# Softmax sums from TensorE over a block of ones, and one reciprocal and product on VectorE for every two window pairs

## The chip, the cores and the metric

The kernel runs on 1 core of one Trainium2 chip. The metric is the device time of one execution in microseconds (us); of several executions the median is given. Engines are named as the profile names them: PE is TensorE's matrix multiply, PEld its weight load, DVE VectorE, ACT ScalarE, POOL GpSimd, SP SyncE, which here only issues DMAs. Everything is computed in float32.

## The reference, cut to what matters

Sixteen images of 128 channels and 32 x 32 points go through a window-attention block (Swin) and then through a convolution block with Fourier transforms. The attention part, on which the change works:

```python
qkv = (t @ qkv_w.T + qkv_b).reshape(-1, N, 3, NH, hd).transpose(2, 0, 3, 1, 4)
q, k, v = (qkv[0], qkv[1], qkv[2])          # N = 64 tokens of a window, 8 heads, hd = 16
attn = jnp.einsum('whnd,whmd->whnm', q * scale, k)
attn = jax.nn.softmax(attn + bias, axis=-1)
out = jnp.einsum('whnm,whmd->whnd', attn, v).transpose(0, 2, 1, 3).reshape(-1, N, C)
out = out @ proj_w.T + proj_b
...
tok = tok + out
t2 = _ln(tok, ln2_g, ln2_b)
t2 = jax.nn.gelu(t2 @ w1.T + b1, approximate=False) @ w2.T + b2
return tok + t2
```

An image has 16 windows of 64 tokens. The second block is a gelu convolution, a pyramid of dilated convolutions, two axis convolutions, a spectral part (rows, turn, columns, product, inverse) and a gated sum of them, followed by an output convolution.

## The kernel before

Each engine has its own instruction stream, written out by hand in program order; the streams meet only at counting semaphores (`wait_ge` before an instruction, `then_inc` behind one). Nothing reorders them. `swin_rest(0)` does the attention block of image 0 alone. Then `both(n, i)` runs 15 times, with i = n + 1: the convolution block of image n and the attention block of image i, interleaved on every engine. `conv_only` ends the program with the convolution block of image 15.

Attention goes over 8 pairs of windows, j = 0 to 7. For one pair:

- PE `scores` (L518) writes 128 x 512 into PSUM bank 2 or 3: partitions are the 64 queries of two windows, columns 8 heads by 64 keys.
- DVE `bias_max` (L957, L960) adds the bias into `score` (three buffers) and takes the row maxima; POOL `less_max` (L1666) subtracts them; ACT `exponent` (L1382) takes exp.
- DVE `row_sums` (L964, L966) sums each head's 64 numbers and takes the reciprocal of the 8 sums; POOL `widen_inverse` (L1677) repeats each reciprocal 16 times into `inv_wide`.
- PE `prob_transposes` (L529) turns the unnormalised exponentials into bank 0, and ACT `prob_copy` (L1387) copies them into `probT` (two buffers).
- PE `values` (L540) multiplies with the values: 8 matrix products of 64 columns, each of which fills 32 partitions of bank 1, so that bank 1 holds four pairs in 512 columns. With every fourth pair ACT `attention_copy` (L1392) copies bank 1 into `attn_out` (its memory is called xw in the trace).

For each half image (four pairs) PE `spread_inverse` (L551) then turns `inv_wide` into bank 2 or 3, DVE `scale_values` (L972) multiplies `attn_out` with it, and PE `project` applies the output projection. DVE `residual_stats` (L978, L918, L921) adds the residual and takes the statistics of the second layer norm, `norm2` (L926, L929) normalises, and PE goes on with transposes (`n2_transposes`) and the MLP.

In `both`, each of the eight steps j has a piece of the convolution block in it. The pieces that matter here: at j = 5 DVE makes the even product (L1117), from which PE computes `inverse_even` (L467, bank 6 and 7) and then `pyramid_conv` (L647, bank 4 and 5); only then come PE's `values(5)`. At j = 6 DVE's `gate_pyramid` (L1139) reads banks 4 and 5 into py, and PE's `inverse_odd` (L467), which writes the same banks, waits for that (semaphore py_sb). `taps` (L1088, L1090) are VectorE's products of the axis convolutions, one 128 x 1024 instruction each, spread over the steps and, nine of them, behind the attention block.

## Time and profile before

| | us |
|---|---|
| median of 3 runs | 1813.92 |
| lowest and highest of them | 1802.71, 1819.46 |
| the profiled execution's own time | 1805.41 |
| its span, from the first instruction to the last | 1803.6 |
| PE busy in the span | 1549.4 (86%) |
| DVE busy | 1364.0 (76%) |
| ACT busy | 864.2 (48%) |
| POOL busy | 684.9 (38%) |

The span is the part that the trace covers; the profiled execution's own time is 1.8 us more. Busy shares are means over stages with different limits, and no engine is busy throughout. The mean granted TensorE clock was 0.953 of full speed.

### The profile page before, as it was taken

What the parts mean: (1) busy time and instruction counts of PE and PEld (TensorE: products, weight loads), DVE (VectorE), ACT (ScalarE), POOL (GpSimd) and SP (SyncE); (2) the same over time, 40 slices, a digit from 0 to 9 for tenths busy, and PEclk for the clock granted to TensorE, in tenths of its full rate; (3) what the DMA queues carried; (4) which work ended last, traced back from release to release, by engine and by line L of the source; (5) the groups of instructions that cost most, each with busy time, mean ns of one, the idle gap of its engine ahead of it and who ended that gap; (6) DMA issues with size and microseconds to landing.
All of it is one profiled execution on the core that took longest, in us unless ns stands there. A gap on an engine that the chain in (4) does not pass through costs nothing.

```text
span 1803.6 us, 32142 instructions
## 1 busy us (share of the span) xinstructions
PE 1549.4 (86%) x11664; PEld 906.3 (50%) x11664; DVE 1364.0 (76%) x2455; ACT 864.2 (48%) x1380; POOL 684.9 (38%) x603
## 2 busy tenths in 40 slices
PE   5789899888989889888998988889888898988884
PEld 3346455464555546445463554546455464555542
DVE  4558778687777878788687777868788786778866
ACT  2344545455454544545455454544545545454533
POOL 3244251634416244251534416134251623416151
PEclk9899999999999999999999999999999999999997
DMA  4011020111102011020111102011020201102020
GB/s 147 1 26 41 26 52 1 43 33 37 39 23 53 0 37 39 25 51 0 43 33 37 39 23 53 0 37 39 25 51 0 58 18 37 39 12 53 0 54 12
DMA packets 19618, 60.23 MB, mean 33 GB/s; under 512 B 6228, under 2 KB 6228, under 8 KB 19204
## 3 DMA queue, kind: packets, MB, share of 16 engines
q1 hardware_dynamic: 19588, 59.83, 13.7%
q8 instruction: 18, 0.29, 0.1%
q14 instruction: 12, 0.10, 0.0%
HBM read 14.04 MB, written 9.02 MB: 13 GB/s over the span
## 4 chain that ended last, share of the span: by engine, by line
DVE 39%; PE 25%; DVEq 16%; issue 7%; ACT 6%; SPq 4%; DMA 3%; ACTq 1%; POOL 0%; POOLq 0%
DVE hv L1090 16%; DVEq L959 7%; DVE nT L929 5%; PE bank L647 5%; PE bank L674 4%; SPq L428 4%; DVE row_max L960 4%; DVEq L965 3%; PE bank L467 3%; PE bank L518 3%; PE bank L489 2%; DMA k_heads<-kC 2%; PE bank L755 2%; DVE score L957 2%; PE bank L577 1%
## 5 line engine op out<-in xcount | busy, mean ns | idle before, releaser
L674 PE MATMUL bank<-act,mats_sb 128*32 128x512 f32 (+11 forms) x2112 | 267.1, 475 | 1.4 <-DVE xs L1026 1.4
L1666 POOL TENSOR_TENSOR score<-score,row_max 128x512 f32<-128x512 f32 x128 | 133.4, 1042 | 306.7 <-DVE row_max L960 305.1
L1350 ACT ACTIVATE fft<-bank 128x512 f32<-128x512 f32 x224 | 168.9, 807 | 125.7 <-PE bank L467 111.8
L1090 DVE SCALAR_TENSOR_TENSOR hv<-hor,mix,hv 128x1024 f32<-128x1024 f32 x128 | 193.8, 1514 | 10.7
L467 PE MATMUL bank<-cons_sb,fft 128*128 128x128 f32 x1280 | 185.4, 306 | 11.8 <-DVE fft L1117 11.8
L1090 DVE SCALAR_TENSOR_TENSOR hv<-ver,mix,hv 128x1024 f32<-128x1024 f32 x144 | 186.9, 1298 | 11.0
L1382 ACT ACTIVATE score<-score 128x512 f32<-128x512 f32 x128 | 80.8, 631 | 225.8 <-POOL score L1666 225.8
L467 PEld LDWEIGHTS bank<-cons_sb,fft 128*128 128x128 f32 x1280 | 172.7, 217 | 31.4 <-DVE fft L1117 17.0
L1677 POOL COPY inv_wide<-row_inv 128x128 f32<-128x128 f32 x128 | 91.8, 717 | 206.7 <-DVE row_inv L966 206.7
L674 PEld LDWEIGHTS bank<-act,mats_sb 128*32 128x32 f32 x2112 | 117.5, 109 | 99.6 <-issue 81.5
L1696 POOL TENSOR_SCALAR hor<-act,cols_sb 128x1024 f32<-128x1024 f32 x16 | 18.0, 1125 | 391.6 <-ACT act L1407 391.6
L518 PE MATMUL bank<-k_heads,qC 128*64 128x512 f32 x512 | 136.1, 621 | 31.8 <-DMA k_heads<-kC 31.8
L577 PE MATMUL bank<-nC,mats_sb 128*128 128x512 f32 x256 | 127.4, 621 | 38.9 <-ACT nC L1350 23.4
L957 DVE TENSOR_TENSOR score<-bank,rel_bias 128x512 f32<-128x512 f32 x128 | 87.2, 681 | 76.3 <-PE bank L518 76.2
L1387 ACT ACTIVATE probT<-bank 128x512 f32<-128x512 f32 x128 | 77.7, 607 | 101.6 <-PE bank L529 101.3
L1706 POOL TENSOR_SCALAR axis_part<-act,cols_sb 128x320 f32<-128x320 f32 (+1 forms) x128 | 109.4, 855 | 22.5 <-issue 22.5
L587 PE MATMUL bank<-fft,mats_sb 128*128 128x512 f32 x256 | 115.2, 593 | 0.0
L1400 ACT ACTIVATE fft<-bank,fold_b 128x512 f32<-128x512 f32 x128 | 79.2, 689 | 68.5 <-PE bank L577 68.5
L929 DVE TENSOR_SCALAR nT<-xT,mv,rstd 128x128 f32<-128x128 f32 x256 | 104.8, 491 | 3.8
L1708 POOL TENSOR_TENSOR ver<-ver,axis_part 128x320 f32<-128x320 f32 (+1 forms) x64 | 100.8, 1575 | 9.4
L960 DVE TENSOR_REDUCE row_max<-score 128x8 f32<-128x512 f32 x128 | 87.8, 686 | 11.6
L577 PEld LDWEIGHTS bank<-nC,mats_sb 128*128 128x128 f32 x256 | 45.1, 191 | 98.2 <-issue 34.4
(180 smaller groups left out, 2903.9 us busy)
## 6 DMA issues: line engine op xcount, KB each, us to landing
pyr_stack<-pyr SPq DMA_DIRECT2D x192, 144.2 KB, 3.1
x_in<-x_dram SPq DMA_DIRECT2D x16, 512.0 KB, 3.5
k_heads<-kC SPq DMA_DIRECT2D x128, 64.0 KB, 2.4
out_dram<-y_out SPq DMA_DIRECT2D x16, 512.0 KB, 2.8
k_heads<-rel_dram SPq DMA_DIRECT2D x2, 1024.0 KB, 13.0
mats_sb<-mats_dram SPq DMA_DIRECT2D x1, 1978.5 KB, 7.4
z_dram<-z_sb SPq DMA_DIRECT2D x32, 19.1 KB
z_run<-z_dram SPq DMA_DIRECT2D x16, 38.2 KB
```

The source lines that it names most:

```text
L467: last = pe.matmul(dst[:, c * P:(c + 1) * P], src[:, at:at + P], rhs, start=True, stop=True)
L518: last = pe.matmul(bank[2 + j % 2][64 * e:64 * e + 64, :], qC[:, w * WT:(w + 1) * WT], k_heads[:, :, w], start=True, stop=True)
L577: pe.matmul(bank[b][:], w_up[:, f * P:(f + 1) * P], nC[:, HALF * k:HALF * k + HALF], start=True, stop=True).then_inc(up_ps, 1)
L587: last = pe.matmul(bank[b][:], w_down[:, f * P:(f + 1) * P], hidden[:, f, HALF * k:HALF * k + HALF], start=False, stop=(f == FC - 1))
L674: last = pe.matmul(grids[32 * d:32 * d + 32, y0 - 16 * k:y1 - 16 * k, x0:x1], w_pyr[:, d, t], act[:, y0 + dy:y1 + dy, x0 + dx:x1 + dx], st ...
L929: last = dve.tensor_scalar(nT[:, c], source[:, c], mv[:, c, 0:1], rstd[:, c:c + 1], ALU.subtract, ALU.mult)
L957: dve.tensor_tensor(score[:, j % 3].rearrange("p h k -> p (h k)"), bank[2 + j % 2][:], rel_bias[:], ALU.add).then_inc(s_biased, 1)
L959: dve.drain()
L960: dve.tensor_reduce(row_max[:, j % 3], score[:, j % 3], AX.X, ALU.max).then_inc(s_max, 1)
L1090: last = dve.scalar_tensor_tensor(hv[:], src, mix[:, a, k:k + 1], hv[:], ALU.mult, ALU.add)
L1350: return act_.activation(dst, src, ACT.Copy)
L1666: pool.tensor_tensor(score[:, j % 3], score[:, j % 3], row_max[:, j % 3].unsqueeze(2).broadcast_to([P, HEADS, WT]), ALU.subtract)\
```

## The change

TensorE computes the softmax sums itself. A constant block `pair` (128 x 32) has ones where the row and the column belong to the same head of a head pair. Behind the 8 value products of a pair stand 4 more products over this block, each of 128 columns, from the same `probT`. Each gives the sum of a head's exponentials, repeated over that head's 16 rows, in the layout of the values. Bank 1 now holds two pairs: columns 0 to 255 the values and columns 256 to 511 the sums.

`scale_values` reads both halves of the bank, once for every two pairs (q = 0 to 3): a reciprocal of 128 x 256 from PSUM into the new tile `inverse`, a drain, and a product of 128 x 256 into `attn_out`. It stands in steps j = 2, 4 and 6 (for q = 0, 1, 2), and for q = 3 behind the residual of the first half. `values` of an even pair waits for the scaling that empties the bank.

`row_sums`, `widen_inverse`, `spread_inverse` and `attention_copy` are gone, with their semaphores. The image loop, the convolution block and the DMAs are as they were.

```diff
             def values(i, j):
                 pe.wait_ge(pT_sb, 8 * i + j + 1)
-                if j == 4:
-                    pe.wait_ge(o_sb, 2 * i + 1)
+                if j % 2 == 0 and j > 0:
+                    pe.wait_ge(o_scaled, 4 * i + j // 2)
+                at = (j % 2) * P
                 for e in range(2):
                     w = 2 * j + e
                     for g in range(HP):
-                        last = pe.matmul(bank[1][32 * g:32 * g + 32, (w % 8) * WT:(w % 8 + 1) * WT],
-                                         v_pair[:, w, g].rearrange("p e d -> p (e d)"),
-                                         probT[:, j % 2, g, e * WT:(e + 1) * WT], start=True, stop=True)
+                        pe.matmul(bank[1][32 * g:32 * g + 32, at + e * WT:at + (e + 1) * WT],
+                                  v_pair[:, w, g].rearrange("p e d -> p (e d)"),
+                                  probT[:, j % 2, g, e * WT:(e + 1) * WT], start=True, stop=True)
+                for g in range(HP):
+                    last = pe.matmul(bank[1][32 * g:32 * g + 32, 2 * P + at:2 * P + at + P], con("pair"),
+                                     probT[:, j % 2, g], start=True, stop=True)
                 last.then_inc(o_ps, 1)
...
-            def row_sums(i, j):
-                dve.wait_ge(s_exp, 8 * i + j + 1)
-                dve.tensor_reduce(row_sum[:, j % 3], score[:, j % 3], AX.X, ALU.add)
-                dve.drain()
-                dve.reciprocal(row_inv[:, j], row_sum[:, j % 3]).then_inc(s_inv, 1)
-
-            def scale_values(i, k):
-                dve.wait_ge(iv_ps, 2 * i + k + 1)
-                dve.wait_ge(o_sb, 2 * i + k + 1)
-                h = slice(HALF * k, HALF * k + HALF)
-                dve.tensor_tensor(attn_out[:, h], bank[2 + k][:], attn_out[:, h], ALU.mult).then_inc(o_scaled, 1)
+            def scale_values(i, q):
+
+                dve.wait_ge(o_ps, 8 * i + 2 * q + 2)
+                dve.reciprocal(inverse[:], bank[1][:, 2 * P:4 * P])
+                dve.drain()
+                dve.tensor_tensor(attn_out[:, 2 * P * q:2 * P * q + 2 * P], bank[1][:, 0:2 * P], inverse[:], ALU.mult)\
+                   .then_inc(o_scaled, 1)
...
                 for j in range(PAIRS):
                     if j + 2 < PAIRS:
                         bias_max(i, j + 2)
-                    row_sums(i, j)
+                    if j in (2, 4, 6):
+                        scale_values(i, j // 2 - 1)
                     if j == 0:
                         route_weights(n)
-                    if j == PAIRS - 1:
-                        scale_values(i, 0)
                     conv_slot(n, j)
                     if j == 3:
                         r_even_bias(n)
                 residual_stats(i, 0)
-                scale_values(i, 1)
+                scale_values(i, 3)
```

The order of the instructions, at the places that the prediction speaks of. First DVE at the end of step j = 5 and in steps 6 and 7, in the loop over images. Names after the arrow are tiles; what a row waits for stands in brackets. Before:

```order
L1090 SCALAR_TENSOR_TENSOR hv<-hor,mix,hv 128x1024
L964 TENSOR_REDUCE row_sum<-score 128x8 [waits s_exp]
L966 RECIPROCAL row_inv<-row_sum 128x8
L1139 SCALAR_TENSOR_TENSOR py<-bank4,cols_sb,axis_part 128x512 [waits pyc_ps,pyramid_mixed,cut_sb]
L1139 SCALAR_TENSOR_TENSOR py<-bank5,cols_sb,axis_part 128x512 [waits pyc_ps]
L1090 SCALAR_TENSOR_TENSOR hv<-hor,mix,hv 128x1024 x2
L964 TENSOR_REDUCE row_sum<-score 128x8 [waits s_exp]
L966 RECIPROCAL row_inv<-row_sum 128x8
L972 TENSOR_TENSOR xw<-bank2,xw 128x512 [waits o_sb,iv_ps]
```

Now:

```order
L1073 SCALAR_TENSOR_TENSOR hv<-hor,mix,hv 128x1024
L952 RECIPROCAL inverse<-bank1 128x256 [waits o_ps]
L954 TENSOR_TENSOR xw<-bank1,inverse 128x256
L1122 SCALAR_TENSOR_TENSOR py<-bank4,cols_sb,axis_part 128x512 [waits pyc_ps,pyramid_mixed,cut_sb]
L1122 SCALAR_TENSOR_TENSOR py<-bank5,cols_sb,axis_part 128x512 [waits pyc_ps]
L1073 SCALAR_TENSOR_TENSOR hv<-hor,mix,hv 128x1024 x4
L961 TENSOR_TENSOR xT<-bank2,resT 128x512 [waits res_sb,proj_ps]
```

The reciprocal and the product of q = 2, which wait for `values` of pairs 4 and 5 (o_ps), stand ahead of the two `gate_pyramid` rows (py). The sums of j = 6 and 7 and the 512-wide product on xw are gone.

Then DVE behind step 7, where the residual of the first half image (xT with bank 2) and the second layer norm are. Before:

```order
L978 TENSOR_TENSOR xT<-bank2,resT 128x512 [waits res_sb,proj_ps]
L918 BN_STATS stats<-xT 128x6 x4
L921 BN_AGGR mv<-stats 128x2 x4
L972 TENSOR_TENSOR xw<-bank3,xw 128x512 [waits o_sb,iv_ps]
L926 RECIPROCAL rstd<-std 128x4 [waits ln2_std]
L929 TENSOR_SCALAR nT<-xT,mv,rstd 128x128 x4
L978 TENSOR_TENSOR xT<-bank3,resT 128x512 [waits res_sb,proj_ps]
L918 BN_STATS stats<-xT 128x6 x4
```

Now:

```order
L961 TENSOR_TENSOR xT<-bank2,resT 128x512 [waits res_sb,proj_ps]
L905 BN_STATS stats<-xT 128x6 x4
L908 BN_AGGR mv<-stats 128x2 x4
L952 RECIPROCAL inverse<-bank1 128x256 [waits o_ps]
L954 TENSOR_TENSOR xw<-bank1,inverse 128x256
L913 RECIPROCAL rstd<-std 128x4 [waits ln2_std]
L916 TENSOR_SCALAR nT<-xT,mv,rstd 128x128 x4
L961 TENSOR_TENSOR xT<-bank3,resT 128x512 [waits res_sb,proj_ps]
```

The product from bank 3 has become the reciprocal and the product of q = 3, at the same place, which waits for o_ps.

Last PE from the end of `pyramid_conv` into step 6. Before:

```order
L647 MATMUL bank5<-pyr_stack,mats_sb 32x512 x12
L540 MATMUL bank1<-probT,v_pair 32x64 [waits pT_sb]
L540 MATMUL bank1<-probT,v_pair 32x64 x7
L467 MATMUL bank4<-cons_sb,fft 128x128 [waits py_sb]
L467 MATMUL bank4<-cons_sb,fft 128x128 x3
L467 MATMUL bank5<-cons_sb,fft 128x128 [waits py_sb]
L467 MATMUL bank5<-cons_sb,fft 128x128 x3
L529 MATMUL bank0<-cons_sb,score 128x128 [waits pT_sb,s_exp]
L529 MATMUL bank0<-cons_sb,score 128x128 x3
L551 MATMUL bank2<-cons_sb,inv_wide 128x128 [waits s_biased,iv_wide]
L551 MATMUL bank2<-cons_sb,inv_wide 128x128 x3
L459 MATMUL bank6<-cons_sb,fft 128x128 [waits ae_sb]
```

Now:

```order
L640 MATMUL bank5<-pyr_stack,mats_sb 32x512 x12
L538 MATMUL bank1<-probT,v_pair 32x64 [waits pT_sb]
L538 MATMUL bank1<-probT,v_pair 32x64 x7
L542 MATMUL bank1<-probT,cons_sb 32x128 x4
L464 MATMUL bank4<-cons_sb,fft 128x128 [waits py_sb]
L464 MATMUL bank4<-cons_sb,fft 128x128 x3
L464 MATMUL bank5<-cons_sb,fft 128x128 [waits py_sb]
L464 MATMUL bank5<-cons_sb,fft 128x128 x3
L526 MATMUL bank0<-cons_sb,score 128x128 [waits pT_sb,s_exp]
L526 MATMUL bank0<-cons_sb,score 128x128 x3
L456 MATMUL bank6<-cons_sb,fft 128x128 [waits ae_sb]
```

Four products of 128 columns follow the values of the pair, and the four products of `spread_inverse` (bank 2, inv_wide) are gone. `inverse_odd` (banks 4 and 5 from fft) still waits for py_sb.

## Rows read from the trace of the kernel before

**Rows 1.** The page's chain that ended last: by engine, by line.

```profile
DVE 39%; PE 25%; DVEq 16%; issue 7%; ACT 6%; SPq 4%; DMA 3%; ACTq 1%; POOL 0%; POOLq 0%
DVE hv L1090 16%; DVEq L959 7%; DVE nT L929 5%; PE bank L647 5%; PE bank L674 4%; SPq L428 4%; DVE row_max L960 4%; DVEq L965 3%; PE bank L467 3%; PE bank L518 3%; PE bank L489 2%; DMA k_heads<-kC 2%; PE bank L755 2%; DVE score L957 2%; PE bank L577 1%
```

**Rows 2.** The waits: who waited for whom, total us, times, longest.

```profile
DVE py L1139 <- PE bank L647: 83.0, 32, 4.1
```

**Rows 3.** Two stretches of one image: busy us of PE, PEld, DVE, ACT, POOL; then clock.

```profile
782.00:812.00 30.00, 25.98 (x232) 15.84 (x232) 27.96 (x44) 14.02 (x23) 17.32 (x16) 0.98 0.26 59
812.00:822.80 10.80, 10.79 (x85) 6.06 (x86) 4.84 (x7) 3.56 (x4) 0.40 (x2) 0.74 0.00 0
```

**Rows 4.** Timeline of DVE in that image: start, duration, line, operation, count.

```profile
810.61 1.35 DVE L1117 TENSOR_TENSOR fft<-fft 128x1024 f32<-128x1024 f32 x1
...
819.60 0.75 DVE L1139 SCALAR_TENSOR_TENSOR py<-bank,cols_sb,axis_part 128x512 f32<-128x512 f32 x1 [4.02 <-PE bank L647]
822.08 0.75 DVE L1139 SCALAR_TENSOR_TENSOR py<-bank,cols_sb,axis_part 128x512 f32<-128x512 f32 x1 [1.73 <-PE bank L647]
822.92 2.64 DVE L1090 SCALAR_TENSOR_TENSOR hv<-hor,mix,hv 128x1024 f32<-128x1024 f32 x2
...
826.46 0.69 DVE L972 TENSOR_TENSOR xw<-bank,xw 128x512 f32<-128x512 f32 x1
827.24 4.43 DVE L1090 SCALAR_TENSOR_TENSOR hv<-hor,mix,hv 128x1024 f32<-128x1024 f32 x2
831.59 0.68 DVE L978 TENSOR_TENSOR xT<-bank,resT 128x512 f32<-128x512 f32 x1
...
833.61 0.66 DVE L972 TENSOR_TENSOR xw<-bank,xw 128x512 f32<-128x512 f32 x1
...
835.51 0.69 DVE L978 TENSOR_TENSOR xT<-bank,resT 128x512 f32<-128x512 f32 x1
```

**Rows 5.** Timeline of PE in that image, matrix products alone.

```profile
812.01 3.78 PE L467 MATMUL bank<-cons_sb,fft 128*128 128x128 f32 x16 [1.02 <-DVE fft L1117]
815.72 6.29 PE L647 MATMUL bank<-pyr_stack,mats_sb 96*32 96x512 f32 x48
821.83 0.40 PE L540 MATMUL bank<-probT,v_pair 128*32 128x64 f32 x16
822.16 2.05 PE L467 MATMUL bank<-cons_sb,fft 128*128 128x128 f32 x16
...
824.49 1.06 PE L551 MATMUL bank<-cons_sb,inv_wide 128*128 128x128 f32 x8
...
829.86 1.06 PE L467 MATMUL bank<-mats_sb,xw 128*128 128x128 f32 x8
```

**Rows 6.** DVE's instruction groups by shape, whole span: busy us, mean ns.

```profile
L964 DVE TENSOR_REDUCE row_sum<-score 128x8 f32<-128x512 f32 x128 | 86.6, 677 | 0.2 <-ACT score L1382 0.2
...
L994 DVE TENSOR_SCALAR xm<-bank,cols_sb 128x256 f32<-128x256 f32 x64 | 26.7, 477 | 17.0 <-PE bank L587 17.0
...
L966 DVE RECIPROCAL row_inv<-row_sum 128x8 f32<-128x8 f32 x128 | 26.0, 203 | 9.4
...
L926 DVE RECIPROCAL rstd<-std 128x4 f32<-128x4 f32 x32 | 5.5, 173 | 5.8 <-ACT std L1346 5.8
...
L926 DVE RECIPROCAL rstd<-std 128x8 f32<-128x8 f32 x16 | 3.3, 204 | 6.6 <-ACT std L1342 6.6
...
L1066 DVE RECIPROCAL vec<-vec 128x1 f32<-128x1 f32 x16 | 2.6, 164 | 1.2
```

**Rows 7.** One-microsecond stretches around that image, columns as in rows 3.

```profile
773.00:774.00 1.00, 0.00 (x0) 0.00 (x0) 1.00 (x1) 0.30 (x1) 1.00 (x1) 1.00 0.57 94
775.00:776.00 1.00, 1.00 (x6) 0.29 (x4) 0.18 (x1) 0.00 (x0) 0.00 (x0) 1.00 0.00 0
871.00:872.00 1.00, 0.12 (x1) 0.12 (x2) 0.82 (x3) 0.00 (x0) 0.85 (x2) 1.00 0.00 0
873.00:874.00 1.00, 1.00 (x3) 0.82 (x4) 0.00 (x0) 0.32 (x1) 0.83 (x2) 0.50 0.00 0
```

54 lines of the change are left out of this document (10 added, 44 removed).

## The prediction

> **What bounds the kernel now.** I read the chain that ended last first. VectorE holds the largest part of it, 39%, with 16% more in its queue (DVEq, mostly drains that wait for the instruction before them); TensorE has 25% [rows 1]. So both matter, and the question is where each leads. The stretches of one image answer it. From 782 to 812 us, steps j = 0 to 5, VectorE is busy 27.96 of 30 us and TensorE 25.98 [rows 3]: VectorE leads, TensorE has 4.0 us to spare. From 812 to 822.8 it is the other way: TensorE is busy throughout and VectorE 4.84 of 10.8 us [rows 3]. The timelines show why. `even_product` starts at 810.61 and TensorE starts `inverse_even` on it at 812.01, then `pyramid_conv` until about 822 [rows 4, 5]. VectorE has little to do meanwhile and waits 4.02 and 1.73 us for the two halves of the pyramid in `gate_pyramid` [rows 4]. Over the program this wait is 83.0 us in 32 waits, two in each of 16 images, so the one image stands for all [rows 2]. Behind it VectorE leads again: its rows to 835.51 follow each other without a gap to speak of [rows 4]. Work on VectorE thus costs time before 810.6 and after 822, and is free between.
>
> **The price of one new scaling.** It is a reciprocal of 256 elements per partition from PSUM, a drain, and a product of 256. The product has a near row: 477 ns for a tensor-scalar of 256 elements out of PSUM [rows 6]; I take 0.45 us. The reciprocal has none of its size. Three of other widths exist: 164 ns for 1 element, 173 for 4, 203 to 204 for 8 [rows 6]. The step from 4 to 8 is 31 ns, 7.7 ns per element, where the row sum takes 677 ns for 512 elements, 1.3 ns each with everything in it [rows 6]. The step from 1 to 4 is only 3 ns per element, so a start-up hides the pace in small ones. At 7.7 ns the reciprocal is 204 + 248 x 7.7 = 2.1 us. The low end of this reading is the mean slope from 1 to 8, 5.7 ns, which gives 1.6 us; the far low end is the pace of the others, 0.45 us (a rival below). The high end is a slope that still grows, 8.5 ns: 2.3 us. I take 2.1, because the widest pair of rows is nearest to 256. One scaling is then S = 2.1 + 0.05 + 0.45 = 2.6 us, with ends 2.1 and 2.8.
>
 The three rows lean towards it, but no row here has a reciprocal long enough to show it.
>
> **What is removed on VectorE.** Eight row sums and reciprocals of 0.68 + 0.20 = 0.88 us [rows 6], 7.0 us per image, and two products of 512, 0.69 and 0.66 us [rows 4]: 8.4 us. Four scalings add 10.4. By totals VectorE gets 2.0 us more per image; by place it is worse.
>
> **Steps 0 to 5.** Six row sums go, 5.3 us, and two scalings come (q = 0 in j = 2, q = 1 in j = 4), 5.2 us. Both wait for values that TensorE finished one step before, so they don't wait. `even_product` starts as it did: 0.0. TensorE has a new wait here: `values(2)` and `values(4)` wait for these scalings, and the next `scores` is queued behind them, for which the next `bias_max` waits. VectorE has other work between (two taps in step 2, `boosted` in step 4), of about the length of `values` and `scores`, so I cost it at nothing; without that cover it would be up to 1 us at each. The added sums on TensorE are 512 columns like the value products, which take 0.40 us for the eight [rows 5]. Half as many instructions, so I take 0.3 us each step, between 0.25 and 0.4. It lies in TensorE's spare 4.0 us.
>
> **The hole at 812 to 822.** Here the change hurts. The sums of pair 6 lay in the hole. What stands there now, the scaling of q = 2, waits for `values(5)`, which TensorE issues only behind `pyramid_conv`: 821.83 + 0.40 + 0.3 = 822.5. And `gate_pyramid` is queued behind the scaling, though its first half was ready at 819.60 [rows 4]. So VectorE idles to 822.5, scales until 825.1, and gates until 826.8 (0.75 us each and a gap), where it ended at 822.83. TensorE's `inverse_odd` waits for the first gate, 825.9, and began at 822.16 [rows 5]: +3.8 us, in which TensorE stands. It gets back `spread_inverse`, 0.89 us from its start to that of the next piece (1.06 with the overlap) [rows 5], and pays 0.3 for the sums of pair 6: project(0), 829.86 to about 830.9 [rows 5], ends at 834.1. VectorE has by then done its taps: 826.8 + 2.64 + 4.43 = 833.8 [rows 4]. The residual of the first half, 831.59 before, starts at 834.1: **+2.5 us**. Two row sums less on VectorE there don't show, as TensorE is the later one.
>
> **Behind it.** Between this residual and the second one stood a product of 0.66 us; now a whole scaling, 2.6, and the second projection waits for it. **+2.0 us.** The second residual thus starts 4.5 us late, and all that follows on both engines hangs on it. The ScalarE copy and `spread_inverse` of the second half, which are gone, lay beside other work there. POOL's `widen_inverse` was on no chain (POOL has 0% of it [rows 1]), so its removal is worth 0.
>
> **The clock.** After idle stretches the granted clock falls to its lower level: TensorE did nothing in 773 to 774 and had full clock at 775, but after 871 to 872, nearly idle, it had 0.50, 1.2 GHz, at 873 [rows 7]. So the same kind of wait is followed by a fall at one time and not at another. What a fall costs is in the timeline: `inverse_even` at the lower level took 3.78 us for 16 records and `inverse_odd` at the upper 2.05 for as many [rows 5]. A fall after the new 3.5 us wait would hit `inverse_odd` and the turns behind it, 3 us of work, so up to +3.0 us in the image. Ends 0 and 3.0; I take 1.5, as the rows show both outcomes.
>
> **Sum.** 15 images with both blocks: 15 x (2.5 + 2.0 + 1.5) = 90 us. Image 0 alone has the same four scalings with less beside them. There the wait of `values(2)` is bare, 2.6 us, the sums add 8 x 0.3, and two `spread_inverse` go: I take +4, with ends 0 and 8. The last block has no attention. 1805.4 + 94 = 1899 us for an execution like the profiled one. The median of the runs is 0.5% above that one (1813.92 to 1805.41), so **1908 us**.
>
> **Rivals.**
> - *The reciprocal is as quick as other instructions* (0.45 us, S = 0.95). Steps 0 to 5 lose 5.3 and gain 1.9, but TensorE has just 4.0 us to give, less 1.8 for six groups of sums, so `even_product` comes 2.2 us early. The gap then costs 0.7 (values and sums) + 0.95 + 0.83 until the first gate, which lands at 822.1, as before; 0.6 us come back by `spread_inverse`, 0.3 go for q = 3. Minus 0.3 to 0.5 per image: 1807 us, not slower than before. It decides at S of about 1.1. If TensorE's denser work in steps 0 to 5 also kept the clock up in `inverse_even` and `pyramid_conv` (0.74 granted in 812 to 822.8 [rows 3]), another 2.7 us per image would go: 1766. For it: nothing in the rows but that the product has this pace. Against it: 31 ns for four elements. The Trainium skill's cycle table (same page, on the errata of SBUF sources) gives VectorE 120 cycles and one per element out of PSUM whatever the operation; by that rule the reciprocal would be 0.39 us, and the rows 4 and 8 elements wide speak against it. 8% for 1807, 4% for 1766.
> - *A slope of 5.7 ns.* S = 2.1: 0.5 less at q = 2 and at q = 3, and up to 1.0 less before the even product. 15 x 4.0 + 4: about 1878. 10%.
> - *The clock falls in every image, and S is 2.8.* 15 x (4.5 + 0.4 + 3.0) + 8 = 127 us: 1941. For it: the wait is the longest of TensorE in the image. 22%.
> - *The four sum products don't run side by side on the array* and take 1.0 us, as 4 of the 128-column products of `spread_inverse` do. 0.7 more at pairs 5, 6 and partly 7: +1.5 us per image, 1931. Against it: eight value products take 0.40 [rows 5]. 5%.
>
> **How the numbers follow.** Forecast 45%, between 1885 and 1925; the rivals as above, 49%; 6% for a gain that I don't see, of one or two per cent. 1850 to 1948 leaves out the quick reciprocal, the unseen gain and the tail of the clock case, some 18% to 20%. A change within 1% can't be told from none here, the runs before differ by 0.9%. Faster by over 1%: 0.06. Within 1%: 0.11. Slower: 0.83.
>
> **What would show it.** In the new profile the 128 x 256 reciprocal should have a mean of 2.1 us (1.6 to 2.3), 64 of them, and the sums 0.3 us a group. VectorE's wait in step 6 should have moved from py to the reciprocal, end with `values(5)`, and TensorE should wait some 3.5 us for py ahead of `inverse_odd`. `even_product` should stand at the same distance from the first `scores`. The prediction is wrong if the reciprocal takes under 1 us, or if TensorE reaches project(0) late by less than 2 us though the reciprocal is long.

## The result, and the profile after

| | before | after |
|---|---|---|
| median, us | 1814.86 | 1939.55 |
| lowest and highest of 4 runs each | 1802.71, 1819.46 | 1930.09, 1947.91 |
| the profiled execution's own time, and its span | 1805.41, 1803.6 | 1937.6, 1935.7 |
| mean granted clock | 0.953 | 0.935 |

The ratio is 1.069 (1.063 to 1.076): the change costs 125 us. The direction was right and the time lies in the range, 32 us above the forecast of 1908 and 8 below the range's upper end. A fourth execution of the kernel before has moved its median from 1813.92 to 1814.86.

The page of the changed kernel: the engines' busy time, and the chain that ended last, by engine and by line.

```profile
PE 1581.2 (82%) x12432; PEld 909.5 (47%) x12432; DVE 1439.5 (74%) x2295; ACT 839.3 (43%) x1348; POOL 665.0 (34%) x475
...
PE 44%; DVE 24%; DVEq 10%; ACT 8%; issue 7%; SPq 3%; DMA 3%; ACTq 1%; POOLq 0%; POOL 0%
PE bank L570 8%; PE bank L464 7%; PE bank L580 6%; DVE nT L916 6%; PE bank L640 4%; DVEq L946 4%; PE bank L515 4%; PE bank L667 4%; SPq L425 3%; PE bank L456 3%; DVE row_max L947 3%; DVE inverse L952 3%; DVEq L953 3%; DVE hv L1073 2%; DMA k_heads<-kC 2%
```

The chain has gone over to TensorE, 44% where it had 25% [rows 1], and its first entry is L570, the MLP's first product (L577 before). TensorE didn't get that much more work, 1581 us against 1549. It waits for VectorE more often (the waits below), and what follows such waits runs in part at a lower clock: the same 256 products of that line took a mean of 621 ns before and take 789 now.

VectorE's groups after, as in [rows 6]: busy us, mean ns of one, idle time before them.

```profile
L952 DVE RECIPROCAL inverse<-bank 128x256 f32<-128x256 f32 x64 | 111.6, 1744 | 86.4 <-PE bank L542 86.4
...
L954 DVE TENSOR_TENSOR xw<-bank,inverse 128x256 f32<-128x256 f32 x64 | 27.2, 425 | 5.1 <-issue 0.4
...
L916 DVE TENSOR_SCALAR nT<-xT,mv,rstd 128x128 f32<-128x128 f32 x256 | 135.6, 611 | 3.8
```

The reciprocal takes 1.74 us, not 2.1, and the product 0.43: a scaling is S = 2.2 us. The third group is one that the prediction didn't look at. The normalisation, L929 before, took 104.8 us with a mean of 491 ns; the same 256 instructions now take 135.6.

The waits after: who waited for whom, total us, times, longest.

```profile
DVE inverse L952 <- PE bank L542: 86.4, 16, 9.0
...
PE bank L464 <- DVE py L1122: 45.6, 15, 3.0
...
PE bank L538 <- DVE xw L954: 40.1, 31, 3.2
...
PE bank L464 <- DVE xw L954: 31.4, 16, 4.3
```

The wait of [rows 2] for the pyramid has gone from py to the reciprocal: 16 waits, one of them in image 0, where no pyramid stands ahead, and one in each of the 15 other images, for `values(5)` with its sums. The others are new, all of TensorE for VectorE: 3.0 us per image ahead of `inverse_odd` (L464 <- py), and others for a scaling.

The gap of one image after, VectorE's timeline, which answers to [rows 4]:

```profile
882.76 1.76 DVE L952 RECIPROCAL inverse<-bank 128x256 f32<-128x256 f32 x1 [5.15 <-PE bank L542]
884.60 0.42 DVE L954 TENSOR_TENSOR xw<-bank,inverse 128x256 f32<-128x256 f32 x1
884.94 1.40 DVE L1122 SCALAR_TENSOR_TENSOR py<-bank,cols_sb,axis_part 128x512 f32<-128x512 f32 x2
886.43 7.31 DVE L1073 SCALAR_TENSOR_TENSOR hv<-hor,mix,hv 128x1024 f32<-128x1024 f32 x4
895.51 0.69 DVE L961 TENSOR_TENSOR xT<-bank,resT 128x512 f32<-128x512 f32 x1 [1.77 <-PE bank L464]
...
897.53 1.73 DVE L952 RECIPROCAL inverse<-bank 128x256 f32<-128x256 f32 x1
...
899.92 3.14 DVE L916 TENSOR_SCALAR nT<-xT,mv,rstd 128x128 f32<-128x128 f32 x4
```

And TensorE's, which answers to [rows 5]:

```profile
858.48 0.43 PE L538 MATMUL bank<-probT,v_pair 128*32 128x64 f32 x16 [0.22 <-DVE xw L954]
...
870.37 0.43 PE L538 MATMUL bank<-probT,v_pair 128*32 128x64 f32 x16 [2.02 <-DVE xw L954]
870.62 0.40 PE L542 MATMUL bank<-probT,cons_sb 128*32 128x128 f32 x8
870.95 1.08 PE L515 MATMUL bank<-k_heads,qC 128*64 128x512 f32 x4
...
874.91 2.05 PE L464 MATMUL bank<-cons_sb,fft 128*128 128x128 f32 x16 [0.34 <-DVE fft L1100]
876.90 5.36 PE L640 MATMUL bank<-pyr_stack,mats_sb 96*32 96x512 f32 x48
882.07 0.41 PE L538 MATMUL bank<-probT,v_pair 128*32 128x64 f32 x16
882.30 0.40 PE L542 MATMUL bank<-probT,cons_sb 128*32 128x128 f32 x8
885.73 2.79 PE L464 MATMUL bank<-cons_sb,fft 128*128 128x128 f32 x16 [3.04 <-DVE py L1122]
...
899.81 1.16 PE L464 MATMUL bank<-mats_sb,xw 128*128 128x128 f32 x8 [1.78 <-DVE xw L954]
903.12 0.66 PE L456 MATMUL bank<-cons_sb,nT 128*128 128x128 f32 x4 [2.15 <-DVE nT L916]
904.55 5.46 PE L570 MATMUL bank<-nC,mats_sb 128*128 128x512 f32 x6 [0.78 <-ACT nC L1332]
```

Read together: VectorE stands 5.15 us until the sums of pair 5 are there, scales, and only then gates the pyramid; `inverse_odd` begins at 885.73, after 3.04 us of waiting. This is what the prediction described. The second place is at 899.92: four normalisations take 3.14 us.

The clock, in the columns of [rows 3] and [rows 7]:

```profile
845.03:875.03 30.00, 26.07 (x266) 16.04 (x264) 28.13 (x36) 11.76 (x20) 15.12 (x10) 1.00 0.26 59
875.03:885.83 10.80, 7.76 (x89) 3.79 (x89) 5.49 (x7) 3.75 (x5) 0.73 (x1) 1.00 0.00 0
...
887.00:888.00 1.00, 1.00 (x7) 1.00 (x6) 0.93 (x2) 1.00 (x1) 1.00 (x1) 0.50 0.00 0
...
905.00:906.00 1.00, 1.00 (x2) 0.36 (x2) 0.56 (x5) 0.89 (x2) 0.00 (x0) 0.50 0.00 0
```

In the gap of this image the clock is now full, 1.00 where it was 0.74 [rows 3], and `inverse_even` takes 2.05 us where it took 3.78 [rows 5]. TensorE waited 0.34 us ahead of it, where it had waited 1.02 [rows 5]. It falls later: to 0.50, 1.2 GHz, at 887 behind the new wait, and at 905 behind the waits for `xw` and `nT`. There the six products of L570 take 5.46 us; their like before, at full clock, took 2.81.

**Where it went, by stretches.** The table cuts an image at instructions that every kernel here has, and gives the mean length of each stretch over the 15 images with both blocks ("tail" and "image": over the 14 that have a next one). "Start" is from the first `scores` to `even_product`, "pyramid" to the end of `pyramid_conv`, "gate" to the end of `gate_pyramid`, "res 1" and "res 2" to the start of the two residuals, "axes" to the first gating of the axis convolutions, "tail" to the next image's first `scores`. It is worked out from the start and end of these instructions in the traces, one execution of each kernel. The kernels e1 to e11 are told below.

| us per image | start | pyramid | gate | res 1 | res 2 | axes | tail | image |
|---|---|---|---|---|---|---|---|---|
| before | 35.90 | 10.88 | 0.83 | 8.75 | 3.93 | 16.20 | 31.65 | 108.2 |
| after | 37.42 | 9.17 | 4.08 | 8.96 | 7.49 | 16.19 | 32.71 | 116.1 |
| e1, copy in place of the reciprocal | 35.38 | 9.57 | 2.75 | 8.14 | 4.19 | 16.20 | 32.51 | 108.8 |
| e2, gate first | 37.28 | 8.89 | 0.82 | 8.20 | 7.49 | 16.19 | 31.76 | 110.7 |
| e3, GpSimd's sum of squares later | 37.97 | 9.33 | 4.09 | 8.87 | 5.56 | 16.20 | 32.34 | 114.4 |
| e4, e2 and e3 | 37.46 | 9.70 | 0.82 | 8.20 | 5.52 | 16.20 | 32.41 | 110.4 |
| e5, sums twice | 38.12 | 8.83 | 4.31 | 9.11 | 7.49 | 16.19 | 33.70 | 117.7 |
| e6, after with 15 reciprocals in the set-up | 37.93 | 9.40 | 4.09 | 8.95 | 7.48 | 16.18 | 33.24 | 117.5 |
| e7, inverse on ScalarE | 40.54 | 9.79 | 0.82 | 9.10 | 5.68 | 16.36 | 32.99 | 115.3 |
| e8, e1 and e2 | 35.82 | 9.78 | 0.82 | 8.19 | 4.19 | 16.20 | 31.96 | 107.0 |
| e9, e4 and a dead reduce | 39.91 | 10.91 | 0.82 | 8.22 | 5.52 | 16.25 | 33.07 | 114.7 |
| e10, before with sums ahead | 37.84 | 10.80 | 0.83 | 8.75 | 3.92 | 16.19 | 30.82 | 109.2 |
| e11, halves | 38.20 | 10.07 | 0.82 | 8.59 | 4.65 | 16.24 | 31.47 | 109.9 |

After minus before is +1.5, -1.7, +3.3, +0.2, +3.6, 0, +1.1: 7.9 us per image, 119 us in 15. Image 0, to the first `scores` of image 1, is 10.9 us longer (137.2 against 126.3). Together 130 of the 132 us between the spans.

**What of it is the clock.** The granted clock falls in some images and not in others, so the same two traces tell most of it apart:

| us | at full clock from end to end | the other images |
|---|---|---|
| start, before | 35.9 (10 images) | 35.9 (5) |
| start, after | 37.0 (11) | 37.3 to 39.4 (4) |
| pyramid, before | none | 10.1 to 11.5 (15) |
| pyramid, after | 8.6 (11) | 9.8 to 12.5 (4) |
| res 1, before | 8.75 (15) | none |
| res 1, after | 8.06 (4) | 9.2 to 10.2 (11) |

So the start is 1.1 us longer without any fall of the clock, and falls add 0.5 in the mean. `res 1` is 0.7 us shorter without a fall, which costs 1.1 us in 11 of the 15 images. "Gate" and "res 2" hardly differ from image to image, whatever the clock. The tail's shortest is 30.8 us in both kernels, and its mean is what falls of the clock in and ahead of it add.

Image 0 after, TensorE's timeline (matrix products of the values and of `project`, L464):

```profile
60.60 0.50 PE L538 MATMUL bank<-probT,v_pair 128*32 128x64 f32 x16 [3.24 <-DVE xw L954]
...
70.60 0.43 PE L538 MATMUL bank<-probT,v_pair 128*32 128x64 f32 x16 [3.24 <-DVE xw L954]
...
78.05 0.65 PE L538 MATMUL bank<-probT,v_pair 128*32 128x64 f32 x16 [1.88 <-DVE xw L954]
...
88.29 2.08 PE L464 MATMUL bank<-mats_sb,xw 128*128 128x128 f32 x8 [4.34 <-DVE xw L954]
```

Nothing covers a scaling there: TensorE waits 12.7 us for the four. `project` takes 2.08 us for the eight records that take 1.06 in [rows 5].

### The profile page after: what moved, and what is told of

Read it like the earlier page. It is cut to its first block, busy times and chain, and to the rows that moved or that the text cites. A ratio compares the mean times of both kernels' runs of the same rounds, so it can differ in the third digit from the quotient of the medians.

```text
span 1935.7 us, 33148 instructions
## 1 busy us (share of the span) xinstructions
PE 1581.2 (82%) x12432; PEld 909.5 (47%) x12432; DVE 1439.5 (74%) x2295; ACT 839.3 (43%) x1348; POOL 665.0 (34%) x475
## 4 chain that ended last, share of the span: by engine, by line
PE 44%; DVE 24%; DVEq 10%; ACT 8%; issue 7%; SPq 3%; DMA 3%; ACTq 1%; POOLq 0%; POOL 0%
PE bank L570 8%; PE bank L464 7%; PE bank L580 6%; DVE nT L916 6%; PE bank L640 4%; DVEq L946 4%; PE bank L515 4%; PE bank L667 4%; SPq L425 3%; PE bank L456 3%; DVE row_max L947 3%; DVE inverse L952 3%; DVEq L953 3%; DVE hv L1073 2%; DMA k_heads<-kC 2%
## 5 line engine op out<-in xcount | busy, mean ns | idle before, releaser
L1638 POOL TENSOR_TENSOR score<-score,row_max 128x512 f32<-128x512 f32 x128 | 184.7, 1443 | 364.8 <-DVE row_max L947 362.7
L464 PE MATMUL bank<-cons_sb,fft 128*128 128x128 f32 x1280 | 178.8, 298 | 50.0 <-DVE py L1122 45.6
L1073 DVE SCALAR_TENSOR_TENSOR hv<-hor,mix,hv 128x1024 f32<-128x1024 f32 x128 | 205.0, 1601 | 10.4
L464 PEld LDWEIGHTS bank<-cons_sb,fft 128*128 128x128 f32 x1280 | 164.2, 208 | 74.3 <-DVE py L1122 49.6
L570 PE MATMUL bank<-nC,mats_sb 128*128 128x512 f32 x256 | 166.9, 789 | 38.9 <-ACT nC L1332 23.4
L952 DVE RECIPROCAL inverse<-bank 128x256 f32<-128x256 f32 x64 | 111.6, 1744 | 86.4 <-PE bank L542 86.4
L667 PEld LDWEIGHTS bank<-act,mats_sb 128*32 128x32 f32 x2112 | 117.5, 109 | 99.6 <-issue 81.4
L916 DVE TENSOR_SCALAR nT<-xT,mv,rstd 128x128 f32<-128x128 f32 x256 | 135.6, 611 | 3.8
L1332 ACT ACTIVATE nC<-bank 128x512 f32<-128x512 f32 x64 | 38.2, 597 | 207.6 <-PE bank L456 207.6
L1680 POOL TENSOR_TENSOR py<-py,xm 128x1024 f32<-128x1024 f32 x16 | 53.2, 3326 | 190.4 <-DVE py L1122 190.4
L570 PEld LDWEIGHTS bank<-nC,mats_sb 128*128 128x128 f32 x256 | 57.7, 243 | 118.0 <-issue 59.6
L1378 ACT ACTIVATE fft<-bank,fold_b 128x512 f32<-128x512 f32 x128 | 80.1, 688 | 74.4 <-PE bank L570 74.2
```

The lines of the kernel that those rows point to most:

```text
L464: last = pe.matmul(dst[:, c * P:(c + 1) * P], src[:, at:at + P], rhs, start=True, stop=True)
L570: pe.matmul(bank[b][:], w_up[:, f * P:(f + 1) * P], nC[:, HALF * k:HALF * k + HALF], start=True, stop=True).then_inc(up_ps, 1)
L667: last = pe.matmul(grids[32 * d:32 * d + 32, y0 - 16 * k:y1 - 16 * k, x0:x1], w_pyr[:, d, t], act[:, y0 + dy:y1 + dy, x0 + dx:x1 + dx], st ...
L916: last = dve.tensor_scalar(nT[:, c], source[:, c], mv[:, c, 0:1], rstd[:, c:c + 1], ALU.subtract, ALU.mult)
L952: dve.reciprocal(inverse[:], bank[1][:, 2 * P:4 * P])
L1073: last = dve.scalar_tensor_tensor(hv[:], src, mix[:, a, k:k + 1], hv[:], ALU.mult, ALU.add)
```

## The experiments

### e1 and e2: is it the length of the reciprocal, or its place?

e1_copy puts a copy of the same block where the reciprocal stood (the division is left out: the values are multiplied by the sums):

```diff
-                dve.reciprocal(inverse[:], bank[1][:, 2 * P:4 * P])
+                dve.tensor_copy(inverse[:], bank[1][:, 2 * P:4 * P])
```

> The changed kernel with the reciprocal of 128 x 256 replaced by a copy of the same block into the same tile, so the division is left out and the output is not scaled. Three theories. (P, place) The loss comes from where the scalings of q = 2 and q = 3 stand: the copy takes 0.42 us where the reciprocal takes 1.74, so 1.3 us go at q = 2, 1.3 at q = 3, up to 1.4 ahead of the even product and perhaps 1 of the clock; the wait of gate_pyramid for values(5) stays. 4 to 5 us per image: 1865 to 1880 us. (L, length) The loss is the reciprocal's length and nothing else: all of it goes, 1815 us or less. (S, sums) The loss is the added products on TensorE: next to nothing changes, 1920 to 1940.

Measured: 1823.03 us, ratio to the kernel before 1.005 (1.002 to 1.008). The copy in e1_copy, from VectorE's groups:

```profile
L952 DVE COPY inverse<-bank 128x256 f32<-128x256 f32 x64 | 26.3, 411 | 92.9 <-PE bank L542 92.9
```

1.33 us less at each of four scalings are 5.3 us per image, and the image got 7.3 shorter: 2.0 in the start, 1.3 in the gate, 0.8 up to the first residual, 3.3 up to the second and 0.2 in the tail, against 0.4 more in the pyramid. So the price by place (1865 to 1880, mine) was wrong, and the theory that all hangs on the length came near. What gives more than its own 1.3 us is the stretch to the second residual, taken up in e3. TensorE's wait for py is still there, 1.7 us in each of the 15 images: a quick inverse alone brings the kernel to half a per cent above the time before, not below it.

e2_gate_first leaves the arithmetic and moves the scaling of q = 2 behind `gate_pyramid`:

```diff
             def conv_slot(n, j, i=None):
...
                 elif j == 6:
                     gate_pyramid(n)
+                    if i is not None:
+                        scale_values(i, 2)
...
-                    if j in (2, 4, 6):
+                    if j in (2, 4):
                         scale_values(i, j // 2 - 1)
```

> The changed kernel with the scaling of q = 2 moved behind gate_pyramid in step 6. Same instructions, same work. Place: gate_pyramid ends 0.8 us behind pyramid_conv as before the change (4.1 now), TensorE's 3.0 us wait for py goes and the fall of the clock behind it with it; 3.3 to 4 us per image, 1880 to 1890 us. Length or sums: nothing is gained by a move, 1930 to 1940, as the scaling only stands 1.6 us later.

Measured: 1856.44 us, ratio 1.025 (1.020 to 1.030). The reciprocal's wait has gone, from 86.4 us to 0.9, as VectorE's groups in e2_gate_first show:

```profile
L952 DVE RECIPROCAL inverse<-bank 128x256 f32<-128x256 f32 x64 | 111.5, 1742 | 0.9 <-PE bank L542 0.9
```

The waits of the same kernel have the one for the pyramid back, with the count of [rows 2]:

```profile
DVE py L1122 <- PE bank L640: 67.9, 32, 3.8
```

The gate stretch is 0.82 us again, as before the change, and the image 5.4 us shorter: 3.3 there, 0.8 up to the first residual, where the clock now stays full in all 15 images, and 0.95 in the tail. This is two thirds of the loss, from one line's place, and more than the 50 to 60 us that I expected. That the length or the sums alone are to blame falls with this run.

e1 says 7.3 us per image and e2 5.4, of 7.9 in all. They don't add, since a short instruction at the wrong place and a long one at the right place each do little harm. e8 below does both.

### e3 and e4: the slow normalisation

The normalisation of the first half (899.92 above) overlaps with GpSimd's instruction of `square_sum`, whose timeline row is:

```profile
900.07 2.39 POOL L1687 TENSOR_TENSOR fft<-fft 128x1024 f32<-128x1024 f32 x1 [10.13 <-ACT fft L1444]
```

One of VectorE's four instructions there took 2.37 us and ended with it. Before, this `square_sum` ran at 836.14 to 838.49 beside the second half's statistics, behind the normalisation at 834.42 that [rows 4] leaves out; the longer scaling has pushed the normalisation onto it. e3_square_late makes GpSimd wait until the normalisation of the first half is done:

```diff
-            def square_sum(n):
+            def square_sum(n, i=None):
+                if i is not None:
+                    pool.wait_ge(n2T_sb, 2 * i + 1)
```

> The changed kernel with one wait more on GpSimd: its sum of squares (128 x 1024, 2.4 us) waits for the first norm2 of the image. In the changed kernel one of the four 128 x 128 normalisations takes 2.37 us where it took 0.3, and ends when GpSimd's sum of squares ends. If the two collide, the four take 1.1 us again instead of 3.1 and the second residual starts 2.0 us earlier: 30 us, 1905 to 1912. Rival: the long normalisation has another cause (the reciprocal ahead of it), then it stays at 2.4 us and the time at 1930 to 1940.

Measured: 1908.89 us, ratio 1.053 (1.050 to 1.057). The normalisation in e3_square_late:

```profile
L916 DVE TENSOR_SCALAR nT<-xT,mv,rstd 128x128 f32<-128x128 f32 x256 | 105.3, 493 | 3.8
```

It has its 493 ns again, the second residual comes 1.9 us earlier per image, and the median is 30.7 us lower, as expected. So of the +3.6 us in that stretch 1.9 are the collision, and the rest is about what the longer scaling costs by itself (2.17 in place of 0.66 is 1.5). The Trainium skill ("SBUF — State Buffer", Who interferes with whom) says that VectorE and GpSimd share one pair of ports as an exclusive lock, and that a tensor-scalar on SBUF can be among those that contend. The trace agrees, with 2.37 us for one instruction of 128 x 128 that ends with GpSimd's.

e4_both_orders has the edits of e2 and e3.

> Both moves together: the scaling of q = 2 behind gate_pyramid, and GpSimd's sum of squares behind the first norm2. Place: the gains add, 5.5 to 6 us per image, 1850 to 1858 us. What is then left against the kernel before is image 0 (some 11 us), 1.6 us per image for the longer scaling of q = 3, and 1.4 us ahead of the even product, less what the clock gives. Rival: if the clock falls at another place in their stead, or one hides the other, it stays above 1875.

Measured: 1852.35 us (1833.70 to 1856.96), ratio 1.019 (1.014 to 1.025). The time is within what I expected, but the 2 us at the second residual, which are there in the table, gave only 0.3 per image over e2, and 4 us by the medians: the pyramid is 0.8 us longer and the tail 0.65. Image 0, in which e4 and e2 are the same, ends 3.6 us later (141.9 against 138.3). The mean clock of the profiled execution is 0.940 against 0.951 in e2, so other falls of the clock have eaten the gain there. That is one execution: the profiled one is the slowest of e4's four, and the fastest, 1833.70 us, had a clock of 0.958. What the second move adds to the first is thus open within some 20 us.

### e5 and e6: the price of the sums, and of a reciprocal

e5_double_sums issues the four sum products of a pair twice:

```diff
-                for g in range(HP):
+                for g in range(2 * HP):
+                    g = g % HP
```

> The changed kernel with each of the four sum products issued twice, the second over the first, so the result is the same. In the changed kernel the sums of a pair put the next product 0.33 us later or less. Place: only the pairs with TensorE ahead of VectorE feel it (5, 6 and 7), 0.25 us each, some 0.7 us per image: 1945 to 1955 us. Sums as a cause of the loss: 8 x 0.3 us per image or more, 1975 us and above.

Measured: 1977.10 us (1966.22 to 1992.82), ratio 1.093 (1.085 to 1.101), 37 us more than the changed kernel by the medians, and 29 by the spans. A group of four products costs 0.33 us in the changed kernel from its start to the next piece (882.30 above follows 882.07; at 870.62 the next `scores` begins at 870.95). Eight groups in 16 images are then 42 us of TensorE time. The table's stretches show 1.6 us more per image, 24 us, and image 0 ends 7.3 us later. How much of that is the sums' own time the totals can't say. e6 below leaves the loop over the images as it was in the changed kernel, and its one execution took 1968.47 us, with 1.4 us more per image and a mean clock of 0.922. That is what falls of the clock can do to a kernel with the same loop, and nearly as much as e5's total.

What is left of e5 without the clock is small. The shortest start is 37.20 us where it was 36.88, the gate is 4.31 in every image where it was 4.08, and `res 1` at full clock is 8.27 where it was 8.06. These are 0.2 to 0.3 us at each of three places, 0.8 us per image, about what I had expected for the place. (The tail's 1.0 us more can't be told apart in this way.) So the prediction's "lies in TensorE's spare 4.0 us" holds nearly: in the start a doubled group in each step costs 0.3 us.

e6_widths puts reciprocals of several widths at the start of the program, each followed by a drain, from SBUF (`boost`) and from PSUM (`bank`), once each:

```diff
+            for width in (1, 2, 4, 6, 8, 12, 16, 32, 64, 128, 256):
+                dve.reciprocal(inverse[:, 0:width], wide[:, 0:width])
+                dve.drain()
```

> The changed kernel with 15 more reciprocals in the set-up, each alone behind a drain: from SBUF at 1, 2, 4, 6, 8, 12, 16, 32, 64, 128 and 256 elements per partition, from PSUM at 1, 8, 64 and 128. It measures the disputed price by itself. The prediction took 7.7 ns an element from the step between 4 and 8 wide; the 256 wide one took 1.74 us. Theory one: a start-up of some 0.2 us and a constant 6.2 ns an element, so 64 wide 0.55 us, 128 wide 0.95, and the source makes no difference but some 50 ns. Theory two: PSUM as a source slows it, then 256 from SBUF differs from 1.74 by more than 0.1 us.

The groups of VectorE in that stretch of e6_widths:

```profile
L1293 DVE RECIPROCAL inverse<-boost 128x256 f32<-128x256 f32 x1 | 1.8, 1753 | 0.1
L1296 DVE RECIPROCAL inverse<-bank 128x128 f32<-128x128 f32 x1 | 1.0, 957 | 0.1
L1293 DVE RECIPROCAL inverse<-boost 128x128 f32<-128x128 f32 x1 | 1.0, 952 | 0.1
...
L1293 DVE RECIPROCAL inverse<-boost 128x64 f32<-128x64 f32 x1 | 0.6, 553 | 0.1
...
L1293 DVE RECIPROCAL inverse<-boost 128x8 f32<-128x8 f32 x1 | 0.2, 202 | 0.1
...
L1293 DVE RECIPROCAL inverse<-boost 128x4 f32<-128x4 f32 x1 | 0.2, 177 | 0.1
```

From 64 elements to 128 it takes 399 ns more, from 128 to 256 801: 6.2 to 6.3 ns per element, and SBUF and PSUM differ by 5 ns. From 4 to 8 the step is 25 ns here, 6.25 each, where [rows 6] gave 31: these rows have means over different places, and a difference of two start-up-bound rows magnified 62 times was a weak base. The Trainium skill ("VectorE: DVE Perf Modes", First, the fixed hardware budget) gives a repeat count of 8, which I had read as 8 cycles per element. By its 0.96 GHz the measured pace is 6.0 cycles, so that reading was a third too high.

### e7 and e8: another way to the inverse, and the change with a quick one

e7_ln_exp computes the inverse on ScalarE, as exp(-ln(sum)), with the gate first as in e2:

```diff
+            def invert(i, q):
+                act_.wait_ge(o_ps, 8 * i + 2 * q + 2)
+                act_.activation(inverse[:], bank[1][:, 2 * P:4 * P], ACT.Ln)
+                act_.drain()
+                act_.activation(inverse[:], inverse[:], ACT.Exp, scale=-1.0).then_inc(inv_sb, 1)
```

> The inverse moves to ScalarE: log of the sums from PSUM, then exp of its negative into the same tile, at the end of steps 1, 3, 5 and 7; VectorE keeps the 256 wide product, and the scaling of q = 2 stands behind gate_pyramid. Full computation. VectorE loses 4 x 1.8 us per image. ScalarE gains 4 pairs of activations and 8 table loads of 1.28 us, as log and the other functions are not in one table. Place: the even product comes up to 2 us earlier than in the changed kernel, and behind the residual the inverse is ready at about the time at which the scaling ended; less than the kernel with gate_pyramid first (1856), 1825 to 1850 us. Rival: ScalarE's loads hold up the copies that TensorE waits for, 1870 us or more.

Measured: 1926.26 us, ratio 1.063 (1.058 to 1.068), where the rival in it had put it (1870 or more). ScalarE's groups at these two lines in e7_ln_exp:

```profile
L1375 ACT ACT_TABLE_LOAD x64 | 82.1, 1283 | 1.2
L1377 ACT ACT_TABLE_LOAD x64 | 82.1, 1283 | 3.3
L1377 ACT ACTIVATE inverse<-inverse 128x256 f32<-128x256 f32 x64 | 26.7, 417 | 0.7
L1375 ACT ACTIVATE inverse<-bank 128x256 f32<-128x256 f32 x64 | 24.6, 384 | 64.5 <-PE bank L543 64.2
```

And who waits for the inverse there, from its waits:

```profile
DVE xw L953 <- ACT inverse L1377: 91.1, 61, 5.4
```

The two functions take 0.80 us, the loads of their tables 2.57: one inverse is 3.4 us, longer than on VectorE, and VectorE waits for it. The rival's mechanism is there too: in the same view TensorE waits 74.4 us for ScalarE's copies at L457 and 40.6 for `probT`, where e2 has 24.7 and 11.3. The start alone is 3.3 us longer than in e2.

e8_copy_gate combines e1 and e2 (again a copy, the division left out).

> The copy in the place of the reciprocal (the division is left out) and the scaling of q = 2 behind gate_pyramid. It bounds what the change could give if the inverse were as quick as other instructions. Place: the two causes, order and length, add in part: from 1856 some 2 us per image go ahead of the even product and 1.3 to 3.3 behind the residual, 1780 to 1800 us, below the kernel before. Length alone: the order gives nothing once the instruction is short, 1815 to 1823.

Measured: 1788.97 us (1778.43 to 1800.45 of 7 runs), ratio 0.987 (0.983 to 0.991), as expected. With the gate first, the reciprocal's length alone costs 3.7 us per image (e2 to e8 in the table). This is the one version that is faster than the kernel before, and it lacks the division. So the form of the change is worth 1.3% if the inverse is as short as a copy and stands behind the gate. It loses its gain because the 128 x 8 reciprocals of the kernel before, 0.20 us for a pair, have become 128 x 256, 1.74 us for two.

### e9 to e11: what stood beside GpSimd's subtraction

The prediction had 0.0 for the start, where 1.5 us were lost, 1.1 of them at full clock. The page shows another group that changed, with not one instruction of it edited: `less_max` on GpSimd. Its group in the changed kernel:

```profile
L1638 POOL TENSOR_TENSOR score<-score,row_max 128x512 f32<-128x512 f32 x128 | 184.7, 1443 | 364.8 <-DVE row_max L947 362.7
```

In the kernel before all 128 took 1041 to 1045 ns. GpSimd subtracts right after the row maxima, and VectorE's next work was then the row sum, beside which the subtraction took no longer. In the changed kernel the next work in steps 1, 3 and 5 is a product of tiles in SBUF, and there both take longer. In steps 2 and 4 it is the reciprocal. Three subtractions in a row after, from GpSimd's timeline:

```profile
968.74 2.38 POOL L1638 TENSOR_TENSOR score<-score,row_max 128x512 f32<-128x512 f32 x1 [0.24 <-DVE row_max L947]
...
972.94 1.04 POOL L1638 TENSOR_TENSOR score<-score,row_max 128x512 f32<-128x512 f32 x1
978.89 2.10 POOL L1638 TENSOR_TENSOR score<-score,row_max 128x512 f32<-128x512 f32 x1 [4.91 <-DVE row_max L947]
```

They alternate: 45 of the 128, three in each of 15 images, take over 2 us. VectorE pays as well. Its instructions in the start apart from the row sums and the scalings are the same in both kernels, and by the traces they are busy 27.0 us per image before and 28.8 after. The Trainium skill ("SBUF — State Buffer", Who interferes with whom) says of trn2 that a tensor-reduce never contends with GpSimd and that a VectorE instruction with two inputs in SBUF does: the trace agrees in both.

e10_before_swap is the kernel before with nothing but the order changed, the row sums ahead of the maxima of the next pair, so that a product follows the maxima:

```diff
-                    if j + 2 < PAIRS:
-                        bias_max(i, j + 2)
                     row_sums(i, j)
+                    if j + 2 < PAIRS:
+                        bias_max(i, j + 2)
```

> The kernel before the change with one swap in the loop over images: the row sums of pair j stand ahead of bias_max of pair j + 2, not behind it. Same instructions. Cover: GpSimd's subtraction now runs beside the products of the convolution block, its mean rises from 1.04 towards 1.4 us, and the even product comes 1 to 2 us later: 1825 to 1845 us. Rival: no cover, the order does not matter, 1805 to 1820 us.

Measured: 1827.83 us, ratio 1.010 (1.005 to 1.016). The subtraction's group in e10_before_swap:

```profile
L1666 POOL TENSOR_TENSOR score<-score,row_max 128x512 f32<-128x512 f32 x128 | 184.9, 1445 | 314.7 <-DVE row_max L960 314.7
```

It has the mean of the changed kernel, and the start is 1.9 us longer (37.84 against 35.90); in 14 of the 15 images the clock is full there up to the last microsecond. VectorE's instructions, the same ones, are busy 2.5 us longer in it, so this is not an engine that waits because of the new order. In step 2, where a 128 x 1024 tensor-scalar of a tap now follows the maxima, the subtraction keeps its 1.04 us and the tap takes 1.54 instead of 0.89: GpSimd's mean shows only a part of such a cost. This shows the cover in the kernel that the change started from.

e9_cover puts it back into e4 the other way: a row sum of `score`, whose result nobody uses, follows the maxima in steps 1, 3 and 5.

```diff
+                    if j in (1, 3, 5):
+                        dve.wait_ge(s_exp, 8 * i + j + 1)
+                        dve.tensor_reduce(row_sum[:, j % 3], score[:, j % 3], AX.X, ALU.add)
+                        dve.drain()
```

> The kernel with both moves (gate_pyramid first, sum of squares late) and, in steps 1, 3 and 5, a sum over the exponentials that nobody reads, put back at the place where the row sum stood. In the changed kernel GpSimd's subtraction of the maxima takes 2.0 to 2.4 us in these steps and 1.04 in the steps where the reciprocal follows the maxima; before the change it took 1.04 in all 128. Theory (cover): VectorE's row sum stood beside the subtraction and does not collide with it, the products on SBUF tiles that stand there now do. Then the subtraction takes 1.04 us again, the products lose some 0.6 us each, and three dead sums of 0.7 us cost nothing or little: 1840 to 1858 us. Rival: the dead sums are simply more work on VectorE, 3 x 0.75 x 15 = 34 us more, 1880 to 1890.

Measured: 1921.81 us, ratio 1.059 (1.055 to 1.064). The subtraction's group in e9_cover:

```profile
L1645 POOL TENSOR_TENSOR score<-score,row_max 128x512 f32<-128x512 f32 x128 | 133.4, 1042 | 438.8 <-DVE row_max L948 438.8
```

GpSimd's 1042 ns are back, where e4 had 1452, and the time is 69 us above e4. Against e4 the start is 2.5 us longer, the pyramid 1.2 and the tail 0.7, at a mean clock of 0.920 against 0.940. That the dead sums cost nothing or little is thus refuted. The traces say why in the start: apart from sums and scalings VectorE's instructions are busy 28.9 us in it, no less than in e4 (28.7), though GpSimd's subtraction is quick again. What one instruction gained another lost (`mix_input` takes 4.4 us where it took 3.9), and the three sums, 2.0 us, came on top. The pyramid is the clock: it fell there in all 15 images, to a mean of 0.79 where e4 has 0.89.

e11_split covers the subtraction with work that has to be done: the reciprocal is split in two of 128 columns, one per pair, behind the maxima of every step. A semaphore keeps the values of the next pair from the bank while VectorE reads it. Both moves of e4 are in it.

```diff
+            def invert(i, j):
+                dve.wait_ge(o_ps, 8 * i + j + 1)
+                at = (j % 2) * P
+                dve.reciprocal(inverse[:, j // 2 % 2, at:at + P], bank[1][:, 2 * P + at:3 * P + at])\
+                   .then_inc(inverted, 1)
...
+                    if 0 < j < 6:
+                        invert(i, j - 1)
```

> Both moves, and the reciprocal split by pairs: 128 wide (0.95 us) once per pair behind the maxima of each step, the product of 256 once per two pairs; the last half stands behind the residual. TensorE's values of an odd pair wait for the reciprocal of the pair ahead, as both use bank 1. Full computation. Cover and place: every subtraction has a reciprocal beside it again (1.04 us), and the second residual comes 0.8 us earlier; the even product has 0.6 to 1.2 us more of scaling ahead of it and 1 to 2 us less of collisions: 1825 to 1850 us. Rival: the new waits of TensorE for half a scaling in every step hold it up by 0.5 us or more each, 1870 and above.

Measured: 1837.93 us (1835.22 to 1850.51), ratio 1.013 (1.009 to 1.017). Its reciprocals, from VectorE's groups:

```profile
L955 DVE RECIPROCAL inverse<-bank 128x128 f32<-128x128 f32 x128 | 121.0, 945 | 2.6 <-PE bank L545 2.6
```

GpSimd's subtraction is at a mean of 1042 ns here too, without dead work, and of all versions of the change with the whole computation this is the quickest, 102 us below the change as it was made. The stretch to the second residual has lost half of its long scaling (4.65 against 5.52 in e4), and the tail is 0.9 us shorter. The start is not shorter than e4's (38.20 against 37.46), though VectorE's instructions apart from the scalings are busy 28.2 us in it instead of 28.7. So the cover is back, but no run shows that it paid in the changed kernel. It is still 1.3% above the kernel before: no version of the change with the division in it beat that one.

## Why the prediction was right, and where not

**The place, right.** The argument on the hole at 812 to 822 held in each step. VectorE stood behind `values(5)` and its sums, `gate_pyramid` behind the scaling, `inverse_odd` behind the gate: 3.04 us of wait where 3.5 were foretold, and 3.3 us more from the pyramid's end to the gates' end where 4.0 were. At full clock the first residual is then 2.6 us late (3.3 less the 0.7 of `res 1`), where 2.5 were foretold; that it is so near is in part luck, as the scaling in that sum was 0.4 us too dear. e2 shows the place by the reverse: with the gate first the 3.3 us are gone to the hundredth.

**The scaling, too dear.** S was given as 2.6 and is 2.17, since the reciprocal goes at 6.25 ns per element and not at 7.7 (e6). The slope from 4 to 8 elements was a difference of two small numbers; the low end of my reading, 1.6 us, was nearer to the measured 1.74 than the 2.1 that I took.

**Steps 0 to 5, "0.0".** They lost 1.5 us, though the two scalings cost 0.9 us less than I counted. The step that failed was to take the six row sums out at their own 5.3 us. They also kept VectorE's products from standing beside GpSimd's subtraction, and this cover went with them: e10 gives it at 1.9 us per image. The changed kernel's own trace has it as 5.3 us of sums less, 4.35 of scalings more, and 1.8 that the unedited instructions of VectorE take longer: +0.9, where the start at full clock is 1.1 longer. The other 0.5 us are the clock, which fell in the start in four of 15 images. TensorE's sums, put into its spare 4.0 us, have no great part (e5: 0.3 us for twice the sums). The waits of `values(2)` and `values(4)`, costed at nothing, are 0.22 us at 858.48 and 2.02 at 870.37 in the image shown, the second twice what I had given as its price without cover; no run shows how much of it comes through to the time. The sign that `even_product` would stand at the same distance from the first `scores` did not come true.

**Behind the first residual, "+2.0".** It is +3.6. The scaling's own excess is 1.5 us (2.17 against 0.66); 1.9 more are the collision of the normalisation with `square_sum` (e3). The prediction read VectorE's queue there and not what GpSimd does at the same time.

**The clock, "+1.5".** From `even_product` to the first residual I had 2.5 + 1.5 = 4.0 us and it is 1.8. The fall after the wait came in 11 of 15 images, as at 887, where `inverse_odd` took 2.79 us instead of 2.05. It costs 1.1 us where it comes, 0.9 in the mean. What I left out of the sum is that the clock no longer falls ahead of `inverse_even` in 11 of 15 images: 1.7 us back in the pyramid, the gain that I had named in a rival alone, as if it needed a quick reciprocal. I had no term for falls elsewhere either: 0.5 us in the start, and those in the MLP, where L570 takes 789 ns instead of 621. The latter are in the stretch "axes", which VectorE bounds and which did not get longer, and come through in the tail, +1.1: with a mean clock of 0.89 in "axes" the tail is 30.8 or 30.9 us (three images after), with 0.68 it is 33.9 to 34.8 (five). Why the clock falls in one image and not in the next with the same instructions no run shows.

**Image 0, "+4".** It is +10.9. I counted one bare wait, and there are four, with the clock at 0.66 in 78 to 100 us where it was 0.95. With the copy (e1) image 1 begins at 127.0 instead of 137.2, so nearly all of it hangs on the reciprocal's length.

**The sum.** 15 x 6.0 + 4 = 94 was forecast, 15 x 7.9 + 10.9 = 130 came. Per image it was too low by 1.5 (start), 1.6 (second residual) and 1.1 (tail) and too high by 2.2 from the even product to the first residual, and in image 0 too low by 7. So the forecast is as near as it is because an error of the clock stands against three others.

**The rivals.** The quick reciprocal was given 1807 us; with a copy it is 1823 (e1): `even_product` comes 0.5 us early (1.0 at full clock), not 2.2, since the cover is gone there too, and the gate still waits. The case of a clock that falls in every image gave the nearest number, 1941 with 7.9 us per image, but by 3.0 us of clock and scalings of 2.8. The fall is 0.9 in the mean and the scaling 2.17, so this nearness is luck. The sum products do run side by side, 0.33 us for four of 128 columns.

## What to carry to other kernels

Before widening a small operation into another layout, price it per element of the free size with a row that is long enough: 8 inverses per partition and pair became 256 for two pairs, and no placement won that back. An instruction that waits should not stand ahead of one that is ready; moving one line here was worth 83 us of 125. And what is removed from an engine may have been the harmless neighbour of another engine's work, so look at what moves up beside it. Where a clock falls in some images and not in others, compare images at full clock first, and do the same with a kernel whose loop was not touched (e6).

## What the runs showed of the hardware

- A float32 reciprocal on VectorE costs 6.25 ns per element and partition from 64 elements up, 1.75 us for 256, from SBUF and PSUM alike; a copy of the same block takes 0.41 us (e6, e1).
- GpSimd's 128 x 512 tensor-tensor takes 1.04 us beside a tensor-reduce or a reciprocal from PSUM and 2.0 to 2.4 beside a product of SBUF tiles (e9, e11, the kernel after). It can also be VectorE alone that pays: a tensor-scalar of 128 x 128 took 2.37 us beside GpSimd's 128 x 1024 product, and one of 128 x 1024 took 1.54 instead of 0.89 beside a subtraction that kept its 1.04 us (e10).
- Where TensorE's clock falls moves with the schedule, and the time with it. In the pyramid it fell in all 15 images before the change and in 4 of 15 after. e6 adds 15 reciprocals (7 us) to the set-up and nothing to the loop, and its single execution took 1968.47 us at a mean clock of 0.922, where the four of the changed kernel took 1930.09 to 1947.91 at 0.928 to 0.940.
